# A selective scan on one core: VectorE reads the step inputs from SBUF, ScalarE uses Silu, four dense banks

## The reference

```python
proj = jnp.einsum('blh,he->bel', input_states, W_in)
hidden, gate = jnp.split(proj, 2, axis=1)
x = lax.conv_general_dilated(hidden, conv_kernel, ...)          # 4 taps, each channel by itself
hidden = jax.nn.silu(x + conv_bias[None, :, None])
...
dt, Bm, Cm = jnp.split(ssm_p, [TR, TR + N], axis=-1)
dts = jax.nn.softplus(jnp.einsum('blr,re->ble', dt, W_dt) + b_dt)
A = -jnp.exp(A_log)
dA = jnp.exp(dts[..., None] * A[None, None])
dBu = dts[..., None] * Bm[:, :, None, :] * hs_ble[..., None]
def step(state, inp):
    a, bu, c = inp
    state = a * state + bu
    y = jnp.einsum('ben,bn->be', state, c)
    return (state, y)
...
y = (scan_out + hidden * D[None, :, None]) * jax.nn.silu(gate)
return jnp.einsum('bel,eh->blh', y, W_out)
```

## Time and profile before

| | |
|---|---|
| time, median of 3 runs | 1177.21 us (1171.12 to 1181.13) |
| the profiled execution's own time | 1177.67 us |
| its span, from the first to the last instruction | 1175.9 us |
| VectorE busy | 973.5 us, 83% of the span |
| TensorE busy | 856.8 us, 73% |
| ScalarE busy | 792.3 us, 67% |
| GpSimd busy | 774.6 us, 66% |
| mean granted TensorE clock, share of full speed | 0.859 |

### The profile page before, as it was taken

How to read it: one execution, slowest core, us unless ns; L and a number is a source line. 1 busy time by engine, 2 the same in 40 slices (tenths; PEclk the granted TensorE clock), 3 DMA queues, 4 the chain that set the end, 5 groups by cost and what they waited for, 6 DMA issues and landing times.

```text
span 1175.9 us, 10334 instructions
## 1 busy us (share of the span) xinstructions
PE 856.8 (73%) x2708; PEld 335.0 (28%) x2718; DVE 973.5 (83%) x783; ACT 792.3 (67%) x1336; POOL 774.6 (66%) x483
## 2 busy tenths in 40 slices
PE   7923488878369789976639789878629856666994
PEld 2311133322023233432214234333203323222331
DVE  2469999898789987888979987898878999999733
ACT  3456677776456886886647777785666677777446
POOL 2228777777567766778656775777666777686533
PEclk9976698889679999998769898998868978777997
DMA  5184444453972334253893343344594353225100
GB/s 177 36 198 104 103 113 110 107 137 86 242 205 67 102 92 108 72 146 83 214 261 77 85 110 80 88 121 108 132 274 102 75 153 91 63 63 143 28 0 37
DMA packets 66684, 135.03 MB, mean 115 GB/s; under 512 B 13120, under 2 KB 19392, under 8 KB 66624
## 3 DMA queue, kind: packets, MB, share of 16 engines
q1 hardware_dynamic: 65904, 134.28, 45.0%
q10 hardware_dynamic: 720, 0.08, 0.0%
HBM read 62.75 MB, written 4.46 MB: 57 GB/s over the span
## 4 chain that ended last, share of the span: by engine, by line
PE 26%; issue 25%; DVE 20%; ACT 15%; DMA 7%; POOL 5%; SPq 1%; DVEq 0%; ACTq 0%; POOLq 0%
PE dense L906 16%; DVE st L804 14%; PE dense L962 6%; ACT dA L589 5%; POOL st L464 4%; DMA rep<-steps 3%; DMA wide<-w_out 3%; DVE dBu L798 2%; PE dense L939 2%; ACT squares L620 1%; DVE hs L782 1%; DVE x L763 1%; ACT L577 1%; ACT du_rep L597 1%; PE dBu L916 1%
## 5 line engine op out<-in xcount | busy, mean ns | idle before, releaser
L464 POOL TENSOR_TENSOR st<-st,Cb 128x1024 f32<-128x1024 f32 x250 | 584.3, 2359 | 216.5 <-DVE st L804 173.7
L804 DVE TENSOR_TENSOR_SCAN st<-dA,dBu 128x1024 f32<-128x1024 f32 x256 | 570.0, 2268 | 0.3 <-ACT dA L589 0.3
L589 ACT ACTIVATE dA<-rep,Aneg 128x511 f32<-128x511 f32 x512 | 328.0, 710 | 84.7 <-DMA rep<-steps 56.4
L798 DVE TENSOR_TENSOR dBu<-du_rep,Bb 128x1024 f32<-128x1024 f32 x250 | 294.4, 1223 | 78.9 <-ACT du_rep L597 46.4
L906 PE MATMUL dense<-xTs,Win 128*128 128x512 f32 x512 | 239.4, 612 | 14.2 <-DMA xTs<-xT 7.8
L939 PE MATMUL dense<-st,sel 128*32 128x512 f32 x1024 | 131.1, 657 | 52.1 <-POOL st L464 52.1
L906 PE MATMUL dense<-wide,hs 128*128 128x512 f32 x256 | 122.0, 633 | 61.9 <-DMA wide<-w_out 39.2
L906 PEld LDWEIGHTS dense<-xTs,Win 128*128 128x128 f32 x512 | 97.6, 195 | 147.3 <-issue 146.6
L962 PE MATMUL dense<-pj,Win 128*128 128x512 f32 (+1 forms) x192 | 105.5, 701 | 34.2 <-DVEq L785 20.7
L597 ACT COPY du_rep<-rep 128x512 f32<-128x512 f32 x128 | 74.3, 581 | 57.0 <-DVE dBu L798 48.6
L503 POOL TENSOR_TENSOR ta<-ta,tb 128x512 f32<-128x512 f32 x32 | 41.1, 1284 | 77.4 <-ACT tb L701 77.4
(11 more groups left out here) (112 smaller groups left out, 845.4 us busy)
## 6 DMA issues: line engine op xcount, KB each, us to landing
rep<-steps SPq DMA_DIRECT2D x512, 128.0 KB, 2.7
Win<-w_in SPq DMA_DIRECT2D x64, 256.0 KB, 2.7
wide<-w_out SPq DMA_DIRECT2D x4, 2048.0 KB, 16.4
Win<-w_conv SPq DMA_DIRECT2D x24, 256.0 KB, 2.6
wide<-bc_rows SPq DMA_DIRECT2D x24, 256.0 KB, 6.3
xTs<-xT SPq DMA_DIRECT2D x4, 1024.0 KB, 10.8
Bb<-bc_rows SPq DMA_DIRECT2D x16, 256.0 KB, 11.1
Cb<-bc_rows SPq DMA_DIRECT2D x16, 256.0 KB, 12.2
```

Of the source, the lines that this page charges most:

```text
L464: nc.gpsimd.tensor_tensor(s, s, C[:, j, :], ALU.mult).then_inc(s_p, 1)
L589: nc.scalar.activation(dA[:, u % 2, j, 1:T], rep[:, u % REPS, 0, 1:T], ACT.Exp, scale=Aneg[:, u % UNITS, j:j + 1]).then_inc(s_dA, 1)
L798: V.tensor_tensor(dBu[:, j, :], du_rep[:].unsqueeze(1).to_broadcast([P, JH, T]), B[:, j, :], ALU.mult).then_inc(s_mul, 1)
L804: V.tensor_tensor_scan(st[:, u % RING, j, :].rearrange("p j t -> p (j t)"), dA[:, u % 2, j, :].rearrange("p j t -> p (j t)"), dBu[:, j, :] ...
```

## The change

VectorE's multiplication reads du where the DMA put it, in `rep`, and no longer from `du_rep`; ScalarE's copy and the bank `du_rep` are gone. The bank that is free becomes a fourth `dense` bank, and `rep` gets a fourth slot. A slot of `rep` is free again when the unit's exponentials and both halves of its multiplication are done (before: exponentials and copy), which SyncE waits for before it issues the next four DMAs into it. Each Silu is one activation, for the hidden input written straight to `hs`, for the gate to `ta`. GpSimd has neither of the two products any more: between its multiplications with C it has only the product for `du`, the additions of a bias and the small operations of the norms. `CONV_AT` writes out the steps of the convolution; they are those that the rule before gave.

```diff
-BANKS = 3
-REPS = 3
+BANKS = 4
+REPS = 4
...
+CONV_AT = [10, 11, 14, 15, 18, 19, 22, 23]
...
-        du_rep = ctx.enter_context(nc.psum_tensor("du_rep", [P, 512], F32))
...
                 if u >= REPS:
                     sp.wait_ge(s_dA, NJ * (u - REPS + 1))
-                    sp.wait_ge(s_duf, u - REPS + 1)
+                    sp.wait_ge(s_mul, NH * (u - REPS + 1))
...
-                for kb, i in pending:
-
-                    pool.wait_ge(s_tanh, 2 * (NE * kb + i + 1))
-                    m = temp[("c" if kb else "h", kb, i)] % TEMPS
-                    nc.gpsimd.tensor_tensor(hs[:, kb % 2, i, :], tb[:, m, :], ta[:, m, :],
-                                            ALU.mult).then_inc(s_hs, 1)
-                    pool.wait_ge(s_hs, NE * kb + i + 1)
-                    pool.sem_inc(s_temp, 1)
-                pending = []
...
-                    elif kind == "g":
-
-                        pool.wait_ge(s_gt, 3 * (n + 1))
-                        nc.gpsimd.tensor_tensor(a, a, t, ALU.mult).then_inc(s_gate, 1)
-                        pool.wait_ge(s_gate, n + 1)
...
             def hid_back(b, i):
                 m = temp[("h", b, i)] % TEMPS
                 act.wait_ge(s_conv, NE * b + i + 1)
-                t = tb[:, m, :]
-                nc.scalar.activation(t, ta[:, m, :], ACT.Tanh).then_inc(s_tanh, 1)
-                act.wait_ge(s_tanh, 2 * (NE * b + i) + 1)
-                nc.scalar.activation(t, t, ACT.Identity, bias=ones[:, 0:1]).then_inc(s_tanh, 1)
+                nc.scalar.activation(hs[:, b % 2, i, :], ta[:, m, :], ACT.Silu).then_inc(s_hs, 1)
...
-                nc.scalar.activation(t, ps, ACT.Tanh, scale=0.5, bias=cb[:, i:i + 1]).then_inc(s_tanh, 1)
-                nc.scalar.activation(a, ps, ACT.Identity, scale=0.5, bias=cb[:, i:i + 1]).then_inc(free, 1)
-                act.wait_ge(s_tanh, n + 1)
-                nc.scalar.activation(t, t, ACT.Identity, bias=ones[:, 0:1]).then_inc(s_tanh, 1)
+                nc.scalar.activation(hs[:, b % 2, i, :], ps, ACT.Silu, bias=cb[:, i:i + 1]).then_inc(s_hs, 1)
+                act.wait_ge(s_hs, NE * b + i + 1)
+                act.sem_inc(free, 1)
...
-            def spread(u):
-
-                act.wait_ge(s_rep[u % REPS], 64 * (u // REPS + 1))
-                if u:
-                    act.wait_ge(s_mul, NH * u)
-                nc.scalar.copy(du_rep[:], rep[:, u % REPS, 1, :]).then_inc(s_duf, 1)
...
-                        nc.scalar.activation(t, ps, ACT.Tanh, scale=0.5).then_inc(s_gt, 1)
-                        nc.scalar.activation(a, ps, ACT.Identity, scale=0.5).then_inc(s_gt, 1)
-                        act.wait_ge(s_gt, 3 * n + 2)
-                        nc.scalar.activation(t, t, ACT.Identity, bias=ones[:, 0:1]).then_inc(s_gt, 1)
+                        nc.scalar.activation(temp_slot(key), ps, ACT.Silu).then_inc(s_gate, 1)
+                        act.wait_ge(s_gate, NE * kb + i + 1)
                         act.sem_inc(free, 1)
...
             def unit(u):
-                dve.wait_ge(s_duf, u + 1)
+                dve.wait_ge(s_rep[u % REPS], 64 * (u // REPS + 1))
...
-                    V.tensor_tensor(dBu[:, j, :], du_rep[:].unsqueeze(1).to_broadcast([P, JH, T]), B[:, j, :],
+                    V.tensor_tensor(dBu[:, j, :], rep[:, u % REPS, 1:2, :].to_broadcast([P, JH, T]), B[:, j, :],
                                     ALU.mult).then_inc(s_mul, 1)
```

More of the change, by code:

```diff
@@ L84, in items @@
         keys.append(("z", (n + 2) // NE, (n + 2) % NE))
[L85 to L88, removed]
+    if after and b >= 0:
+        keys.extend(("c", b + 1, i) for i, at in enumerate(CONV_AT) if at == g)
+    if after:
+        keys.extend(("h", b + 1, i) for i, at in enumerate(HID_AT) if at == g)
     if b >= 1:
@@ L122, in decoder_layer @@
     turn = {key: (n % BANKS, n // BANKS) for n, key in enumerate(order)}
-    temp_keys = [key for key in order if key[0] in "gc" or key[0] == "h" and key[1] == 0]
+    temp_keys = [key for key in order if key[0] == "g" or key[0] == "h" and key[1] == 0]
     temp = {key: m for m, key in enumerate(temp_keys)}
@@ L165, in decoder_layer @@
         ta = sb("ta", [P, TEMPS, T])
-        tb = sb("tb", [P, TEMPS, T])
         pj = sb("pj", [P, T])
@@ L239, in decoder_layer @@
         s_conv = sem("conv_done")
-        s_tanh = sem("tanh_done")
-        s_temp = sem("temp_free")
         s_hs = sem("hs_ready")
@@ L249, in decoder_layer @@
         s_du = sem("step_inputs_ready")
-        s_gt = sem("gate_part")
         s_gate = sem("gate_ready")
         s_rep = [sem(f"rep_loaded{i}") for i in range(REPS)]
-        s_duf = sem("du_rep_full")
         s_dA = sem("dA_ready")
@@ L485, in _ @@
                     n = NE * kb + i
[L486 to L489, removed]
+                    if kind == "z":
                         pool.wait_ge(s_dt, n + 1)
+                        pool.wait_ge(s_hs, n + 1)
                         nc.gpsimd.tensor_tensor(steps[:, n % 3, 1, :], steps[:, n % 3, 0, :], hs[:, kb % 2, i, :],
@@ L531, in temp_slot @@
                     else:
-                        act.wait_ge(s_temp, sum(k[0] != "g" for k in temp_keys[:m - TEMPS + 1]))
-                return ta[:, m % TEMPS, :], tb[:, m % TEMPS, :]
+                        act.wait_ge(s_hs, i + 1)
+                return ta[:, m % TEMPS, :]
             def hid_front(b, i):
                 ps, _ = full(("h", b, i))
-                a, _ = temp_slot(("h", b, i))
-                if b == 0 and i == 0:
-                    act.wait_ge(s_prep, 1)
+                a = temp_slot(("h", b, i))
+                if i == 0:
+                    act.wait_ge(s_conv_c, 32)
                 nc.scalar.activation(a, ps, ACT.Identity, scale=ck[:, i, KC - 1:KC],
@@ L585, in exps @@
                     if u < 2:
-                        act.wait_ge(s_prep, 2)
+                        act.wait_ge(s_prep, 1)
                 if u >= 2:
@@ L657, in _ @@
                     first = NJ * (UNITS * b + g + 1)
-                    u = first // NJ
-                    if u == 0:
-                        spread(0)
                     for m in range(first + AHEAD if first else 0, min(first + NJ + AHEAD, NB * UNITS * NJ)):
                         exps(m // NJ, m % NJ)
-                    if u + 1 < NB * UNITS:
-                        spread(u + 1)
                 for args in pending:
@@ L695, in _ @@
                         ps, free = full(key)
-                        a, t = temp_slot(key)
-                        n = NE * kb + i
-                        nc.scalar.activation(t, ps, ACT.Tanh, scale=0.5).then_inc(s_gt, 1)
-                        nc.scalar.activation(a, ps, ACT.Identity, scale=0.5).then_inc(s_gt, 1)
-                        act.wait_ge(s_gt, 3 * n + 2)
-                        nc.scalar.activation(t, t, ACT.Identity, bias=ones[:, 0:1]).then_inc(s_gt, 1)
+                        nc.scalar.activation(temp_slot(key), ps, ACT.Silu).then_inc(s_gate, 1)
+                        act.wait_ge(s_gate, NE * kb + i + 1)
                         act.sem_inc(free, 1)
@@ L829, in _ @@
             dve.wait_ge(s_conv_c, 32)
-            link(V.tensor_scalar(ck[:], ck[:], 0.5, None, ALU.mult))
-            V.tensor_scalar(cb[:], cb[:], 0.5, None, ALU.mult).then_inc(s_prep, 1)
             link(V.memset(dA[:, :, :, 0:1], 0.0))
```

3 lines of the change are left out of this document (removed).

## The result

The changed kernel takes 1306.73 us (median of 4 runs, 1306.41 to 1308.07), against 1178.8 us for the kernel before (the median of the three runs shown above and a fourth): the ratio is put at 1.111, 95% interval 1.1064 to 1.1156 (the two medians alone give 1.109). Of all the runs here one, of the experiment *The copy, earlier*, fell in a slow state, 1532.55 us at a granted clock of 0.551, and is left out of every comparison.

The account below looks back on a forecast made before the run. VectorE was taken to bound a third of the units without slack. From 1177.7 us, 173 (hold) and 10 (du product) were added, 20 (longer gaps) and 6 (ahead of the loop) taken off: 1335 us, range 1130 to 1395.

Parts of the forecast that it names:

- What bounds: VectorE in the loop: the bound without any slack in a third of the units, 6.61 us a unit.
- The hold: VectorE's multiplication from SBUF waits for GpSimd's second half: 2.37 us late, 173 us over 98 gaps; chance 0.60.
- the du product: GpSimd's product behind every fourth unit can hold the multiplication: 10 us taken, 41 if always, otherwise nothing.
- The 29 longer gaps: VectorE's gaps above 2.37 us, 60 us above it in all: 20 us of gain taken, of 0 to 60.
- The step ahead of the loop: Eight additions of one in a pace-setting ScalarE and VectorE chain, and the first unit's copy, go: 6 us less.
- The copy's waits: VectorE's waits for the copy to PSUM: 38.6 of 49.4 us go, but under the hold most buys nothing.
- The no-hold rival: Two SBUF inputs cost VectorE nothing beside GpSimd and the copy's waits go: 1133 us (1115 to 1165), chance 0.23.
- ScalarE: 155.8 us of work gone, 97.5 us of table loads added, 58 us less; nothing taken, bounds 0 and 14.
- GpSimd's products for Silu: They leave a GpSimd queue that has room; no gain was taken for them.
- The fourth bank: Lets TensorE run one product further ahead; counted as part of the 60 us in the longer gaps.

Follow-up runs that it names:

- The copy, earlier: Changed kernel with the copy to PSUM and three dense banks back, the copy set between the two halves of the exponentials: 1165.29 us, ratio 0.9919.
- the operand alone: Kernel before (Tanh, three banks, three slots) with only the copy taken out and the multiplication reading rep: 1332.71 us, ratio 1.1338.
- the short product: Changed kernel with GpSimd multiplying only 4 of each 512 columns with C: 1135.97 us in one run.
- the memsets: Changed kernel with GpSimd filling the same columns with ones instead of multiplying them with C: 1140.17 us in one run.
- the first experiment: Changed kernel with the copy to PSUM put back, with three dense banks and SyncE's wait for the copy: 1172.56 us, ratio 0.9975.
- GpSimd behind the multiplications: Changed kernel with GpSimd's products with C waiting until both halves of the next unit's multiplication are done: 1250.8 us, ratio 1.0642.

## Why the prediction was right, step by step

*What bounds.* VectorE bounds a third of the units without slack, so a longer multiplication shows in full: right. In the 43 units whose gap was below zero, the pairs grew by 98 us in all and the gaps stayed as they were.

*The hold.* The step rested on four rows of another instruction, L756 beside two products of GpSimd; that the multiplication would be held as L756 was is my estimate, which no row of the kernel before shows. It took the price from the end of GpSimd's second product less 0.2 us, 2.37. Measured, the pair went from 2.34 to 4.71: 2.37. The variant named with it, that GpSimd's second product slips in between the halves, is what happens. That the sizes agree to 0.01 us is partly luck: by the windows above VectorE waited 0.33 us for the rest of the first product and 2.19 for the second, 2.52 where the prediction had 2.57, and 0.16 us passed under the hold where it had 0.2. Three experiments show the cause: the loss goes with the operand (the copy put back, 1172.6 us), comes with the operand alone (1332.7) and goes with GpSimd's reads (the short product, 1136.0).

The runs show what the multiplication from SBUF is held by: it takes 2064 ns in the mean beside products, which read SBUF, and 1274 beside memsets of the same columns, which only write it. The hold is a turn for each instruction: 1.45 us of delay for a pair beside products of 512 columns, 2.37 beside those of 1024.

*The terms.* Unit by unit, the 98 with gaps below 2.37 us became 169.3 us longer. The prediction had 173 for the hold and 10 for the du product. The 29 longer gaps, with their pairs, gave back 36.0 us; the prediction took 20 of 0 to 60. So the sum was too long by some 14 us in the first, 16 in the second and, against that, short by 3 us ahead of the loop: 6 predicted, 3.3 measured. The rest of the distance to 1335 is the 1.1 behind the loop. The step ahead of the loop was misread: of the eight steps there only the first few (4.56 us each before) were paced by ScalarE and VectorE. ScalarE's timeline ahead of the loop, now:

```profile
31.06 0.78 ACT L519 ACTIVATE ta<-dense,cb,ck 128x512 f32<-128x512 f32 x1 [1.54 <-PE dense L859]
...
36.53 0.78 ACT L519 ACTIVATE ta<-dense,cb,ck 128x512 f32<-128x512 f32 x1 [1.54 <-PE dense L859]
```

A step takes 36.53 - 31.06 = 5.47 us, as the later steps did before, and ScalarE waits 1.54 us of it for TensorE (0.79 before): the addition of one that went there became a longer wait. So the last of the eight activations starts only 0.26 us earlier (50.75 against 51.01 us). What came earlier lies behind it: ScalarE's next copy, which waits for TensorE's product of their results, starts at 52.60 instead of 54.95 us, now that neither the addition nor GpSimd's product stands in between. How much of the 3.3 us is the change's and how much the run's stays open: kernels above with this same beginning start their loop between 67.5 and 70.6 us.

*The du product* was mis-sized. It was feared to hold VectorE for up to 1.29 us in each of 32 units. The pair at 100.64, with the du product at 104.22, took 4.71 us, as did the pair at 109.64 without one: VectorE's second half, which already waited, went first, and the du product was held instead (2.25 us, 1829 ns in the mean, where it had 1271). The reason given for a small value was right, and 10 should have been nothing in this kernel; where the du product comes first it does hold, as beside the memsets (3.42 us).

*The copy's waits.* That they buy little was right: VectorE waits for no copy now, and the 38.6 us went into gaps that the hold fills. The no-hold rival's 1133 us counted all of them as gained. The short product comes near it (1136.0), but there most of GpSimd's own work is gone too, and *The copy, earlier*, in which GpSimd does all of its work unhindered, speaks against that sum: 35.4 us less of waiting for the copy made the gaps only 6.3 us shorter. What no hold would have given with all of GpSimd's work, no run shows.

*ScalarE* has 139 loads, as counted:

```profile
L561 ACT ACT_TABLE_LOAD x62 | 79.5, 1283 | 52.1 <-DVE st L760 48.6 <-ACT ta L656 2.5 <-ACT steps L549 0.6
...
L549 ACT ACT_TABLE_LOAD x31 | 39.8, 1283 | 0.6
L538 ACT ACT_TABLE_LOAD x24 | 30.8, 1283 | 1.6
...
L656 ACT ACT_TABLE_LOAD x20 | 25.7, 1283 | 1.2 <-ACT small L669 0.5 <-ACT xTs L682 0.3 <-ACT small L682 0.2
```

(two more stand ahead of the loop). But its busy time fell by 32.5 us, not 58. Its instructions' durations, added up over the whole trace, did fall as predicted, from 875.1 to 816.5 us. But back to back they overlap, and busy time counts an overlap once: four exponentials of 710 ns take 2.56 us in a row (the last line below), 0.09 less for each that follows another. With 248 instructions gone this overlap fell from 82.8 to 56.8 us, the missing 26. A table load doesn't overlap, as in the earlier trace rows: here it ends at 98.62 + 1.28 = 99.90 us, and the exponentials start at 99.91.

```profile
98.62 1.28 ACT L561 ACT_TABLE_LOAD   x1 [3.40 <-DVE st L760]
99.91 2.56 ACT L561 ACTIVATE dA<-rep,Aneg 128x511 f32<-128x511 f32 x4
```

That this costs nothing on the path was right, by the first experiment.

*GpSimd's products for Silu* were put at nothing, as work in a queue that has room. For a kernel without the hold that is so (the copy put back, 3 us). Under the hold Silu with their removal, and the fourth slot, are worth 22.5 us (1332.71 against 1310.17), and the pairs of multiplications, in which the hold lies, are some 30 us shorter. GpSimd was busy for 69% of the span in the slower of the two, and its instructions still cost time there, since they also stopped VectorE.

*The fourth bank* under the hold: some 3 us or nothing, where the prediction gave it a part of what the longer gaps give back.

## What to carry to other kernels

Before an operand moves from PSUM to SBUF, look at what GpSimd reads at that moment: a VectorE instruction with two SBUF inputs and a GpSimd instruction with an SBUF input ran one after the other here, and that cost 2.4 us a unit where the copy it replaced was hidden but for 39 us in all. A stray pair of rows can show such a hold elsewhere in the same trace, if one asks which instruction takes twice its time and whose end it ends with. A producer that is late is better moved earlier in its own engine's order (here some 6 us gained) than removed at the price of such a hold; and where two engines must be kept apart, the small operations that others wait for go ahead of the wait.

## What the runs showed that I had not expected

Even a GpSimd instruction of one column can be held: the norms' power of one column went from 552 to 1163 ns in the mean (550 with the copy put back), the 8-column product from 0.20 to 1.10 us. In the changed kernel:

```profile
L475 POOL TENSOR_TENSOR steps<-steps,hs 128x512 f32<-128x512 f32 x32 | 58.5, 1829 | 51.7 <-ACT steps L549 51.7
L464 POOL TENSOR_TENSOR rstd<-var,neghalf 128x1 f32<-128x1 f32 x48 | 55.8, 1163 | 34.0 <-ACT var L588 34.0
```

The turns alternate strictly in the rows seen: no engine got two instructions in while the other waited, so the length of an instruction decides the other's wait (3.37 us for a multiplication beside a 1024-column product). And an order that removes the collision, GpSimd behind the multiplications, gave back 56 us where 112 to 157 had been expected from its pace, since 48 pairs of tiny instructions stood in the same queue.
